# Context rows turned by two 16-bit DMA transposes with Pool at both ends, in place of TensorE transposes, from the fifth group on

## What is computed

```
x, ctx: (8, 256, 512) float32
qh = layernorm(x) as (8, heads 8, d 32, 512);  kh = vh = ctx as (8, 8, 32, 512)
s = log(itok[b]) / (8 * log 20)
attn = softmax(s * einsum('bhdq,bhdk->bhqk', qh, kh))
x = x + einsum('bhqk,bhdk->bhdq', attn, vh)
y = layernorm(x); x = x + sum of the top-2 of 8 experts(y) + 0.2 * shared(y)
```

## Time and profile before

| | us |
|---|---|
| median of 3 runs | 1350.37 |
| lowest and highest | 1350.11, 1351.13 |
| profiled execution, its own time | 1353.0 |
| its span, first to last instruction | 1351.2 |
| PE busy | 1305.0 |
| DVE busy | 839.0 |
| ACT busy | 704.5 |
| Pool busy | 250.8 |

### The profile page before, as it was taken

How to read it: one execution, slowest core, us unless ns; L and a number is a source line. 1 busy time by engine, 2 the same in 40 slices (tenths; PEclk the granted TensorE clock), 3 DMA queues, 4 the chain that set the end, 5 groups by cost and what they waited for, 6 DMA issues and landing times.

```text
span 1351.2 us, 26893 instructions
## 1 busy us (share of the span) xinstructions
PE 1305.0 (97%) x11055; PEld 950.2 (70%) x11072; DVE 839.0 (62%) x1408; ACT 704.5 (52%) x1056; POOL 250.8 (19%) x219
## 2 busy tenths in 40 slices
PE   5788999999999999999999999999999999999997
PEld 2143646556464737375788889999999988888895
DVE  7777768778778787765552844728456284472730
ACT  4757675757676666673332533535344353442521
POOL 4540000000001041433200311203012030120012
PEclk9899999999999999999999999999999999999999
DMA  9514141222356223324826757767576675767413
GB/s 273 183 55 125 33 110 48 83 67 71 79 72 70 84 67 102 98 52 72 266 94 134 196 141 188 170 141 197 145 201 147 139 198 142 186 145 152 95 25 40
DMA packets 182572, 165.08 MB, mean 122 GB/s; under 512 B 104889, under 2 KB 125513, under 8 KB 182450
## 3 DMA queue, kind: packets, MB, share of 16 engines
q1 hardware_dynamic: 170162, 138.15, 39.0%
q0 software_dynamic: 12288, 25.21, 10.9%
HBM read 109.47 MB, written 34.15 MB: 106 GB/s over the span
## 4 chain that ended last, share of the span: by engine, by line
PE 86%; DVE 4%; ACT 4%; issue 3%; POOL 1%; DMA 0%; POOLq 0%; ACTq 0%; DVEq 0%
PE banks L1821 25%; PE banks L1851 24%; PE banks L1755 11%; PE banks L1737 10%; PE banks L1677 4%; PE banks L1657 4%; PE banks L1625 3%; DVE rowmax L1281 2%; ACT hidden L1058 1%; ACT QS L1045 1%; PE banks L1711 1%; PE banks L1686 1%; PE banks L1862 1%; PE banks L1723 1%; POOL w1l L942 1%
## 5 line engine op out<-in xcount | busy, mean ns | idle before, releaser
L1851 PE MATMUL banks<-hidden,w2h 128*128 128x0 bf16 x2048 | 306.1, 269 | 0.0
L1058 ACT ACTIVATE hidden<-banks,scales 128x512 f32<-128x512 f32 x256 | 171.1, 686 | 101.5 <-PE banks L1657 86.4
L1851 PEld LDWEIGHTS banks<-hidden,w2h 128*128 128x128 bf16 x2048 | 198.6, 98 | 20.5
L1281 DVE TENSOR_REDUCE rowmax<-banks 128x1 f32<-128x512 f32 x256 | 172.5, 684 | 40.3 <-PE banks L1625 38.3
L1851 PE MATMUL banks<-hidden,w2l 128*128 128x0 bf16 x1024 | 192.3, 269 | 0.0
L1432 DVE TENSOR_TENSOR w1l<-stage,w1h 128x2048 bf16<-128x2048 f32 x32 | 73.2, 2291 | 186.3 <-ACT w1h L1135 186.3
L1755 PE MATMUL banks<-w2h,hidden 128*128 128x512 bf16 x512 | 184.3, 379 | 0.0
L1152 ACT ACTIVATE hf<-banks,b1cols 128x640 f32<-128x640 f32 x128 | 101.1, 790 | 123.1 <-PE banks L1821 107.7
L1163 ACT ACTIVATE yT<-banks 128x640 uint16<-128x640 uint16 x56 | 36.3, 701 | 215.3 <-PE banks L1851 215.3
L1821 PE MATMUL banks<-eth,w1h 128*128 128x0 bf16 x1024 | 133.0, 273 | 0.0
L1821 PE MATMUL banks<-eth,w1l 128*128 128x0 bf16 x1024 | 132.9, 273 | 0.0
(11 more groups left out here) (198 smaller groups left out, 1970.4 us busy)
## 6 DMA issues: line engine op xcount, KB each, us to landing
stage<-in_L_ffn_w SPq DMA_DIRECT2D x64, 1024.0 KB
split_parts<-hidden SPq DMA_DIRECT2D x16, 512.0 KB, 5.8
QS<-split_parts SPq DMA_DIRECT2D x48, 128.0 KB, 2.7
KS<-split_parts SPq DMA_DIRECT2D x48, 128.0 KB, 3.1
xin<-in_x SPq DMA_DIRECT2D x16, 256.0 KB, 3.7
cin<-in_ctx SPq DMA_DIRECT2D x16, 256.0 KB, 3.6
out_rows<-xin SPq DMA_DIRECT2D x16, 256.0 KB, 2.0
normed_rows<-x2r SPq DMA_DIRECT2D x16, 256.0 KB, 3.2
```

Source lines behind the costliest of these rows:

```text
L1058: ac.activation(prob[n % NPH], bank(score_bank[unit]), ACT.Exp, scale=scales[:, g // 2:g // 2 + 1]).then_inc(s_exp, 1)
L1281: dv.reduce_max(rowmax[g % 2][:, i:i + 1], bank(score_bank[unit]), X_AXIS).then_inc(s_max, 1)
L1851: issued = mm(bank(b0 + j)[:, skips[j]:CAP].shape_from_register(used_cols(e, j)), w[:, fb, rows], of_choice(a[:, fb, :], j, skips[j]).shap ...
```

## The change

For w = 0 nothing changes. From w = 1 on, for groups 4 to 15, `turn_v` is gone and two units stand for it. `split_v` is at step 0 (group a + 2) and step 6 (a + 3): Pool copies `cin`, read as 16-bit numbers two apart, to `planes` (low halves, then high halves), and SP turns each plane by a transposing DMA into `turned_v`. `join_v` is at steps 5 and 11: Pool interleaves the turned planes again into `VT`. There is one `planes` and one `turned_v`, in the space of `b2f` and `wuf` made 128 partitions high. The loads for a + 4 stay at step 3.

```diff
-            if more and n in (2, 3):
+            if more and w == 0 and n in (2, 3):
                 add("turn_v", a + n)
-                if a + 4 < GROUPS and n == 3:
-                    add("load", a + 4)
-                    add("c_load", a + 4)
+            if more and w and n in (0, 6):
+                add("split_v", a + 2 + n // 6)
+            if more and w and n in (5, 11):
+                add("join_v", a + 2 + n // 6)
+            if n == 3 and a + 4 < GROUPS:
+                add("load", a + 4)
+                add("c_load", a + 4)
...
+                elif kind == "split_v":
+                    g = unit[1]
+                    sp.wait_ge(s_vt, g + 1)
+                    sp.wait_ge(s_vtc, g)
+                    for a in range(2):
+                        dma(turned_v[:, a, :].rearrange("p (t c) -> p t c", c=P), planes[:, a, :], transpose=True).then_inc(s_vturn, 16)
...
+                elif kind == "split_v":
+                    g = unit[1]
+                    pool.wait_ge(s_c[g % 2], 16 * (g // 2 + 1))
+                    if g == NS:
+                        pool.wait_ge(s_b2, 1)
+                    else:
+                        pool.wait_ge(s_vturn, 16 * 2 * (g - NS))
+                    gp.tensor_copy(planes, cin[g % 2][:, :].bitcast(U16).rearrange("p (c a) -> p a c", a=2)).then_inc(s_vt, 1)
+                elif kind == "join_v":
+                    g = unit[1]
+                    pool.wait_ge(s_vturn, 16 * 2 * (g - NS + 1))
+                    pool.wait_ge(s_pv, QT * (g - 1))
+                    if g == NS:
+                        pool.wait_ge(s_wuc, 1)
+                    gp.tensor_copy(VT[g % 2][:, :].bitcast(U16).rearrange("p (c a) -> p a c", a=2), turned_v).then_inc(s_vtc, 1)
...
-                        pe.wait_ge(s_vtc, g + 2)
+                        pe.wait_ge(s_vtc, min(g + 2, NS))
```

More of the change, by code:

```diff
@@ L482, in build @@
         wdh, wdl = sb("wdh", [P, KB, WIDE], BF16), sb("wdl", [P, KB, WIDE], BF16)
-        wuf, wus = sb("wuf", [WIDE, D], F32), sb("wus", [P, D], BF16)
+        wuf_turned, wus = sb("wuf_turned", [P, D], F32), sb("wus", [P, D], BF16)
+        wuf = wuf_turned[0:WIDE, :]
+        turned_v = wuf_turned[:, :].bitcast(U16).rearrange("p (a c) -> p a c", a=2)
         hidden = sb("hidden", [P, 2 * FB * SLOTS], BF16)
@@ L500, in build @@
         sb1rows, sb1cols = sb("sb1rows", [FB, P], F32), sb("sb1cols", [P, FB], F32)
-        b2f = sb("b2f", [E + 1, D], F32)
+        b2f_planes = sb("b2f_planes", [P, D], F32)
+        b2f = b2f_planes[0:E + 1, :]
+        planes = b2f_planes[:, :].bitcast(U16).rearrange("p (a c) -> p a c", a=2)
         b2parts = sb("b2parts", [E + 1, 3, D], BF16)
@@ L615, in build @@
         s_stack = [sem(f"s_stack{i}") for i in range(NS)]
-        s_vt, s_vtc = sem("s_vt"), sem("s_vtc")
+        s_vt, s_vtc, s_vturn = sem("s_vt"), sem("s_vtc"), sem("s_vturn")
         s_score, s_max, s_ms, s_rows, s_row = (sem(n) for n in ("s_score", "s_max", "s_ms", "s_rows", "s_row"))
```

## The result

The changed kernel took 1355.67 us (median of 6 runs, 1353.69 to 1357.12) beside 1350.24 us (6 runs, 1346.71 to 1351.13) for the kernel before: ratio 1.0044, 95% interval [1.0034, 1.0055]. A second set of runs of the same kernel gave 1358.97 against 1350.86, ratio 1.0059 [1.0043, 1.0076]. The forecast was +13.1 us; measured are +5.4 and +8.1. The profiled execution took 1355.9 us, its span is 1354.1.

What follows compares the result with a forecast made beforehand. PE was taken to set the pace (72.70 of 73.3 us busy), with DVE full for 8 us; 4 x 2.80, window 1 +1.91 and window 6 -0.04 gave +13.1 us, hence 1363.5 us, range 1349 to 1373.

Steps and rivals of the forecast that it cites:

- What PE and ACT lose: Turns leave PE, 0.93 us a window, 5.6 us in all if nothing else binds; ACT's 12 copies of 0.588 count nothing.
- rival 1: No block: Pool's copies do not hold up DVE, the turns simply leave PE; 6 x 0.89 = 5.3 us, 1345.0; chance 0.12.
- The mechanism: Each Pool copy blocks DVE's operations with two SBUF inputs by up to c, not the maxima, which read PSUM; PE waits.
- the price c of a copy: Duration of one Pool copy of 1024 16-bit elements a partition: estimated 1.7 us, with 0.94 and 2.3 kept for the range.
- window 6: It has no group a + 4; its join falls in DVE's idle stretch, so it was left at -0.04 us.
- place 2: Join of a + 2 and split of a + 3, steps 5 and 6: DVE +3.02 us, PE's score at 309.73 +2.80.
- Rival 2: Short copies, c = 0.94: score +0.52 us a window, +1.7 in all, 1352.0, no change; chance 0.18.
- Rival 3: Long copies, c = 2.3: PE +0.56 us after place 1, score +4.78, +22.8 in all, 1373.1; chance 0.10.
- Place 1: Split of a + 2 at step 0: sum L1302 1.10 us late, PE's ones +0.89, after the turns PE at -0.04.
- What was hidden: Step 11's join, landings, SP's order and the delayed load of xin (about 295.0) count nothing; cover left some 2 us.
- Rival 5: xin late: transposes take 7.2 us, statistics come 1.5 us late on a full DVE; 1371 us; chance 0.03.
- Rival 4: DVE keeps its turn at place 2, L1408 ahead of the split: score +1.60 us, +7.1 in all, 1357.5; chance 0.17.

Runs made afterwards that it cites:

- experiment 2: The changed kernel with Pool's copies cut from 512 to 2 columns of each plane, only the first split whole: 1346.54 us, ratio 0.9968.
- experiment 4: The changed kernel with all work kept, Pool's copies moved to where DVE idles or takes maxima, xin's load ahead of the transposes: 1345.98 us, ratio 0.996.
- experiment 3: The changed kernel without the transposing DMAs, the join reading planes that are not turned, copies kept: 1360.1 us, ratio 1.0076.
- experiment 8: The kernel before, TensorE's turns and ACT's copies kept, with Pool's four unused copies a window added at the change's places: 1362.87 us, ratio 1.0097.
- experiment 6: The changed kernel with only the split of step 0 whole (and the first split), the other copies cut to 2 columns: 1350.26 us, ratio 1.0018.
- experiment 7: The changed kernel with only the pair at steps 5 and 6 whole (and the first split), others cut to 2 columns: 1350.03 us, ratio 1.0005.

## Why the prediction was right in direction and wrong in size

**What PE and ACT lose: right.** The turns take 0.93 us a window by the earlier trace rows, of which rival 1 expected 0.89; experiments 2 and 4 show windows 0.89 and 0.91 us shorter. Rival 1, the case without a block, stood at 1345.0, 5.3 us less than before; the two kernels without a block took 1346.5 and 1346.0, 4.3 and 4.9 less.

**The mechanism: right, with one kind of victim missing.** The copies hold up DVE's instructions with two SBUF inputs, not the maxima, and PE then waits for the maximum; experiments 2, 3 and 8 leave nothing else. The earlier trace rows was the right row to lean on. The prediction's list of victims lacks the casts from one SBUF tile to another, which have one input: they are held in windows 5 and 6 (below) and by the memsets.

**The step that failed is the price c of a copy.** The prediction took "c = 0.09 + 8 x 0.20 = 1.7 us" from a cast of 128 elements in the earlier trace rows. A copy alone takes 1.04 (split) and 1.34 us (join). What one cast of 128 elements took was mostly not per element: 0.29 us for 128 and 1.04 for 1024 are 0.75 us for 896 elements, 0.83 ns each, if the cast and the split go at one rate, and then the fixed part is 0.18 us and not 0.09. Experiment 2's copies of 4 elements agree: undisturbed they take 0.18 us. The prediction's own steps with the measured 1.04 and 1.34 for 1.7 put the ones at +0.23, the join to 306.27, L1330 to 306.86, the split to 307.90 and the score of 309.73 at +1.11 (window 1 +0.89, window 6 -0.70): 4 x 1.11 + 0.89 - 0.70 = +4.6 us instead of +13.1, where +5.4 and +8.1 came. So c alone accounts for most of the miss. The true split lies next to the memset's 0.94, the bound that I kept as the low end.

At place 2, "DVE late on arrival +0.22, join +1.10, split +1.70, together +3.02" became +0.24, +0.49 and +0.84, together +1.57. The first is read so: the window stands 0.77 us later by the start of the x2r sum (290.65 for 289.88 in the earlier trace rows), and L1359 starts 1.01 us later (306.99 for 305.98), so DVE has lost 0.24 within the window. Less the slack of 0.22 the three leave 1.35; the score of step 10 starts 2.12 us later (311.85 for 309.73), of which 0.77 is the window's shift, and that leaves 1.35 too. The window grew by 1.39. The prediction had only this score waiting; that of step 9, with 0.54 us of slack before, waits first (0.72), and step 10 adds 0.16. The step was right in form; as DVE feels them here, c is 0.84 us for the split and, with the 0.60 us of the maximum that it runs beside, 1.09 for the join. At step 0 the same split holds DVE 1.26 us, more than the 1.04 that it takes alone; why is open.

**Rival 2, short copies, was the nearest case in c** (0.94) and gave +0.52 a window and 1352.0. That is below what came, since the join takes 1.34 and not 0.94, and since it shares the next error. **Rival 3** is 0.2 us a window too high even by its own price: its join at 306.38 leaves out DVE's 0.19 us of idle time, which the forecast took off.

The Trainium skill, "GPSIMD Engine Reference", section "7. Performance pitfalls for Q7 kernels", would make 1.62 us of its 1.9 cycles per element, an estimate; the section "3.1 Elementwise — side-by-side cycle accounting" would make 0.88 us of its 1.03 cycles, an estimate too. The split's 1.04 us is nearer to the second, the join's 1.34 nearer to the first.

**Place 1: wrong instruction, wrong first victim.** "Pool is free at 289.36 + 0.87": the copy starts 0.61 us after the DMA instruction ahead of it, not 0.87. So it and the x2r sum (L1348, now L1377) come at the same moment, Pool goes first, and L1377 is held 1.26 us, where I had the sum behind it held 1.10. "PE's ones wait for it": before them PE's score of step 2 waits for its maximum, 295.61 + 0.61, and starts at 296.36, 1.75 us later than before, of which 0.77 is the window's own shift. It had 0.27 us of slack against 1.26 us of hold: in the kernel before the score starts 1.02 us after its maximum (293.59, 294.61). I had checked only the ones. With the right c and my order, place 1 would have cost 0.23 us instead of the 1.04 of experiment 6. The overpriced c hid this: the forecast of -0.04 after the turns lies near what came, +0.11 (the ones at 297.61 for 295.80, less the shift of 0.77 and the turns' 0.93).

**Windows 1, 5 and 6.** Window 1 has no sum at step 0 and its place 1 is free, as foretold (L1377 0.69 us). In w = 5 the split met the cast ahead of the sum instead: 2.06 us for 0.42, held 1.64, 0.38 more than the sum's 1.26; that window lost 0.47 more than the others. Against Pool's DMA instruction the cast starts only 0.07 us later than in w = 3 (439.47 to 439.62 there, 290.12 to 290.20 here), so little decides who is held. DVE's two rows of w = 5:

```profile
439.62 2.06 DVE L1372 CAST x2r<-x 128x512 bf16<-128x512 f32 x1
441.72 0.69 DVE L1377 TENSOR_TENSOR x2r<-x,x2r 128x512 bf16<-128x512 f32 x1
```

Window 6 was forecast at -0.04 and came at -0.03, but that is luck: the forecast had a hold of 1.10 us on a sum, by the too high c, delay the ones. Pool is late there, behind its own work for the routing, and the split runs beside another cast with one SBUF input:

```profile
518.13 1.60 DVE L1419 CAST low<-lowf 96x256 bf16<-96x256 f32 x1
518.50 1.08 POOL L952 COPY b2f_planes<-cin 128x1024 uint16<-128x1024 uint16 x1
...
520.97 0.39 PE L1654 MATMUL banks<-KS,QS 96*128 96x512 bf16 x1 [0.89 <-DVE rowmax L1310]
```

The cast took 0.51 us in the kernel before, the score of step 2 waits 0.89, and this eats the window's gain: from the mark of w = 5 to that of w = 6 it is 72.85 us, 72.95 with the first split alone (experiment 6) and 71.87 without long copies (experiment 2).

**What was hidden: right.** The landing (2.5 us), SP's order and the load of `xin` took no time (experiment 3); the load of window 3 is issued at 295.69, 294.92 without the shift, where about 295.0 was forecast, and no row of DVE waits for it. The join of step 11 took none either (experiments 6 and 7). Rival 5 (`xin` late) and rival 3 (long copies) fall. Rival 4, DVE keeping its turn at step 6, gave 1357.5 with c = 1.7, a time close to what came, but for another reason: the split did go ahead of L1437, for the join had held L1359 and the split was next.

## What to carry over

When work moves to Pool beside a full DVE, count each Pool instruction that reads SBUF as a block on DVE's instructions with two SBUF inputs, and any long one, even a memset, as a block on DVE's casts between SBUF tiles. Look for where DVE idles or reads PSUM: the same four copies cost 2.3 us a window at one place and nothing at another, and this, not the choice of engine, decided between 0.4% slower and 0.4% faster. Price an operation that the trace lacks with the fixed part taken out by two sizes, not by multiplying the smallest row. And of an engine that falls behind, ask for every reader in order of time; the first to wait sets the loss, and time lost on PE before DVE's idle stretch is not won back in it.

## What the runs showed of the chip that I had not expected

- Pool's and DVE's claims come in single instructions. Cut in two, the join and the split cost DVE 0.51 us instead of 1.33 at steps 5 and 6: the first half of the join is done when the maximum that it runs beside is (both by about 305.7 us). At step 0 both halves ran in a row all the same.
- A memset on Pool, which reads nothing, stretches DVE's cast from 0.41 to 2.04 us, and leaves its subtractions and the sum L1359 alone. A copy holds casts up too, 2.06 us for 0.42 in window 5 and 1.60 for 0.51 in window 6, though they have one SBUF input.
- A Pool copy follows a DMA instruction's start on Pool by 0.61 us, though the DMA is shown as 0.87 us long.
- Separating 1024 16-bit numbers takes Pool 1.04 us, interleaving them 1.34: writing two apart costs 0.3 us more than reading two apart (experiment 4).
